# Layer 0 of a four-layer graph network on one core: the strips of the count table built in another order and at another pace

## What is computed

```
h = relu(layernorm(x));  x = x + L0(h)   # sum over edges of (h @ W[edge type])[src], 16 types, + bias + h @ W_loop
h = relu(layernorm(x));  x = x + L1(h)   # [h, sum over edges of h[src]] @ W.T + b
h = relu(layernorm(x));  x = x + L2(h)   # an MLP on every edge (h[src], h[dst], edge features), mean per node
h = relu(layernorm(x));  x = x + L3(h)   # sum over edges of [h[src], edge features] @ W1, then a last product
```

## Time and profile before

| | us |
|---|---|
| median of 3 runs (4931.5 to 4936.65) | 4932.48 |
| the profiled execution, its own time | 4949.62 |
| its span, first to last instruction | 4947.3 |
| busy in the span: PE, DVE, ACT, POOL | 3938.6, 2813.5, 2195.5, 3564.0 |
| layer 0's gathers by POOL: first start, last end | 254.2, 2138.48 |
| the count table: first quad, last quad | 463.0, 2118.7 |

### The profile page before, as it was taken

The page is one execution under the profiler, slowest core; times in us unless marked ns, Lnnn a source line. Parts: engine busy times, 40 slices in busy tenths (PEclk is TensorE's granted clock), DMA queues, the critical chain, the costliest instruction groups (busy, mean ns, idle before and its releaser), DMA issues. The chain is left out here.

```text
span 4947.3 us, 75766 instructions
## 1 busy us (share of the span) xinstructions
PE 3938.6 (80%) x24234; PEld 2678.4 (54%) x24249; DVE 2813.5 (57%) x7266; ACT 2195.5 (44%) x3840; POOL 3564.0 (72%) x3738
## 2 busy tenths in 40 slices
PE   6755677777788777749996688888889999999876
PEld 3354566555444443434543566666666666666643
DVE  7576999977666666643433332234445555666434
ACT  4510257767778888820111333333333333333300
POOL 6777577777777777757770677777777777777756
PEclk9855567878776778769997777789899999999888
DMA  8821223444344344448883323334445556666376
GB/s 278 325 55 36 55 89 121 132 134 130 122 133 132 120 146 132 135 117 294 279 274 119 85 80 80 80 108 130 122 133 146 157 165 170 175 170 177 98 212 175
DMA packets 580950, 719.66 MB, mean 145 GB/s; under 512 B 138104, under 2 KB 463580, under 8 KB 569952
## 3 DMA queue, kind: packets, MB, share of 16 engines
q1 hardware_dynamic: 394526, 509.02, 31.2%
q0 software_dynamic: 118064, 176.98, 14.9%
q10 hardware_dynamic: 67986, 28.96, 2.2%
HBM read 502.83 MB, written 217.42 MB: 146 GB/s over the span
## 5 line engine op out<-in xcount | busy, mean ns | idle before, releaser
L1356 POOL DMA_INDIRECT layer_msg<-snd_table,idx_src x1536 | 1461.3, 951 | 587.3 <-issue 458.0
L1356 POOL DMA_INDIRECT layer_msg<-rel_table,idx_rel x1440 | 1399.5, 972 | 495.2 <-issue 427.5
L1623 ACT CAST early_room<-layer_unit_ps 128x700 fp8e4<-128x700 f32 (+5 forms) x1371 | 1115.6, 884 | 483.2 <-PE layer_unit_ps L2337 368.3
L2277 PE MATMUL layer_sum_ps<-layer_sel,layer_msg 128*97 128x24 f32 (+21 forms) x6560 | 896.5, 283 | 393.1 <-DVE layer_hidden_acc L1820 150.3
L2337 PE MATMUL layer_unit_ps<-layer_hot_room,layer_low_hot 128*128 128x350 bf16 (+6 forms) x5172 | 940.9, 327 | 318.5 <-ACT early_room L1623 201.6
L2277 PEld LDWEIGHTS layer_sum_ps<-layer_sel,layer_msg 128*128 128x128 f32 (+2 forms) x6560 | 882.6, 208 | 515.5 <-issue 268.7
L2337 PEld LDWEIGHTS layer_unit_ps<-layer_hot_room,layer_low_hot 128*128 128x128 bf16 x5172 | 445.9, 124 | 732.5 <-ACT early_room L1623 550.7
L1808 DVE TENSOR_TENSOR layer_msg<-layer_pre_ps,layer_msg 128x512 f32<-128x512 f32 x392 | 270.9, 691 | 958.3 <-DMA layer_msg<-snd_table,idx_src 878.7
L1944 DVE TENSOR_SCALAR layer_hot_room<-count_iota,frame_key 128x686 bf16<-128x686 f16 (+6 forms) x2586 | 699.7, 336 | 0.0
L2260 PEld LDWEIGHTS layer_pre_ps<-layer_rcv,layer_sel_t 128*128 128x128 f32 x3144 | 476.0, 217 | 228.6 <-issue 228.6
L1356 POOL DMA_INDIRECT layer_msg<-h_table,idx_src x416 | 401.3, 965 | 181.9 <-issue 121.4
(11 more groups left out here) (290 smaller groups left out, 4028.8 us busy)
## 6 DMA issues: line engine op xcount, KB each, us to landing
counts<-early_room SPq DMA_DIRECT2D x48, 1543.5 KB
layer_unit<-counts SPq DMA_DIRECT2D x120, 441.0 KB
rel_table<-first_rows SPq DMA_DIRECT2D x98, 512.0 KB
layer_attr<-in_edge_attr_dram SPq DMA_DIRECT2D x766, 64.0 KB
layer_piece<-counts SPq DMA_DIRECT2D x24, 1575.0 KB
layer_rcv<-rcv_table SPq DMA_DIRECT2D x396, 64.0 KB
counts<-early_room SPq DMA_DIRECT2D x16, 1568.0 KB
layer_msg<-snd_table,idx_src POOLq DMA_INDIRECT x1536
```

The lines of the kernel that those rows point to most:

```text
L1356: nc.gpsimd.indirect_dma_start(msg[g][:, u, 0:2 * D if dense else width], None, of, bass.IndirectOffsetOnAxis(ap=idx[:, at:at + 1], axis=0 ...
L1623: nc.scalar.copy(to[:, :, col:col + w].rearrange("p (v h) c -> p v h c", v=2), of.rearrange("p v (h c) -> p v h c", c=w), saturate=False). ...
L2277: last = nc.tensor.matmul(sum_ps[g % 2][0:rows, 0:span], msg[g][:, u, 0:rows], sel[j][:, u, 0:span], start=u == 0, stop=u == TILES - 1)
```

## The change

Three things change, all of them in the lists that are made before the program is written out.

- `interleave` puts the strips into a new order. They are parted at strip 41 into two queues; whichever engine, DVE or ACT, has had less than its share of its own whole time so far gets strips from the queue that suits it, two at a time (strips 1 to 3 one at a time). Strip 0 stays first.
- `number` counts tiles in the new order; a tile's place in the edge lists (its slot, `SLOT_OF`) stays as it was, so that the gathers of the lists and the table in HBM are the same. A quad is now up to four tiles with neighbouring slots: 650 quads where there were 647.
- The weight of a unit comes from the time of DVE and of ACT by the two formulas.

```
+def vector_time(frames):
+    return sum(tiles * (0.37 + 0.024 * width) for width, tiles, _, _ in frames)
+
+def scalar_time(frames):
+    return 0.2 * -(-sum(width for width, _, _, _ in frames) // WIDEST) + 0.0955 * sum(f[0] for f in frames)
+
+def interleave(strips):
+    ahead, behind = list(range(1, len(strips) // 2)), list(range(len(strips) // 2, len(strips)))
+    taken = []
+    times = [[of(frames) for _, _, frames in strips] for of in (vector_time, scalar_time)]
+    whole = [sum(time[1:]) for time in times]
+    while ahead or behind:
+        spent = [sum(time[k] for k in taken) for time in times]
+        queue = behind if behind and (not ahead or spent[0] * whole[1] > spent[1] * whole[0]) else ahead
+        take = 1 if queue[0] < 4 else 2
+        taken += queue[:take]
+        del queue[:take]
+    taken.insert(0, 0)
+    return [strips[k] for k in taken]
...
-            weight = [sum(tiles * (3 * width + 11) for width, tiles, _, _ in held) +
-                      6 * sum(width for width, _, _, _ in held) + 12 for _, held in UNITS]
+            loads = [(vector_time(held), scalar_time(held)) for _, held in UNITS]
+            whole = [sum(load[e] for load in loads) for e in range(2)]
+            shares = [(load[0] / whole[0], load[1] / whole[1]) for load in loads]
+            weight = [max(0.85 * max(pair), sum(pair) / 2) for pair in shares]
...
-                    at = tiles[0] + (LIST_GAP if tiles[0] >= HEAD_TILES else 0)
+                    at = SLOT_OF[tiles[0]]
```

More of the change, by code:

```diff
@@ L99, in lay_out @@
 def lay_out():
-    panels, strips, frames, runs, node, tile, at, gap = [], [], [], [], 0, 0, 0, 0
+    panels, strips, runs, node, at, slot = [], [], [], 0, 0, 0
     for n, (cols, shapes) in enumerate(PANEL_STRIPS + TAIL_STRIPS):
         if n == len(PANEL_STRIPS):
-            node, gap = TAIL_NODE, -tile % P
+            node, slot = TAIL_NODE, -(-slot // P) * P
         panels.append((cols, len(shapes), node, at))
         for shape in shapes:
-            begin, col = len(frames), 0
+            frames, col = [], 0
             for width, tiles, count in shape:
@@ L112, in lay_out @@
                 else:
-                    runs.append((node, width, tiles, count, tile + gap))
+                    runs.append((node, width, tiles, count, slot))
                 for _ in range(count):
-                    frames.append((width, tiles, col, tile))
-                    col, node, tile = col + width, node + width, tile + tiles
+                    frames.append((width, tiles, col, slot))
+                    col, node, slot = col + width, node + width, slot + tiles
             assert col == cols <= STRIP_COLS
-            strips.append((cols, at, begin, len(frames)))
+            strips.append((cols, at, frames))
@@ L119, in lay_out @@
             at += P * HI * cols
-    return panels, strips, frames, runs, tile, at, gap
-PANELS, STRIPS, FRAMES, RUNS, COUNT_TILES, TABLE, LIST_GAP = lay_out()
+    return panels, strips, runs, at, slot
+def vector_time(frames):
[15 more added lines that the diff above has]
+    return [strips[k] for k in taken]
@@ new lines, in number @@
+def number(laid):
+    strips, frames, slots = [], [], []
+    for cols, at, held in laid:
+        begin = len(frames)
+        for width, tiles, col, slot in held:
+            frames.append((width, tiles, col, len(slots)))
+            slots += range(slot, slot + tiles)
+        strips.append((cols, at, begin, len(frames)))
+    quads = []
+    for tile, slot in enumerate(slots):
+        if quads and len(quads[-1]) < TILES and slots[quads[-1][-1]] + 1 == slot:
+            quads[-1].append(tile)
+        else:
+            quads.append([tile])
+    return strips, frames, slots, quads
@@ L124 @@
+PANELS, LAID, RUNS, TABLE, LISTED = lay_out()
+STRIPS, FRAMES, SLOT_OF, QUADS = number(interleave(LAID))
+COUNT_TILES = len(SLOT_OF)
 HEAD_PANELS = len(PANEL_STRIPS)
-HEAD_TILES = FRAMES[STRIPS[sum(len(shapes) for _, shapes in PANEL_STRIPS)][2]][3]
-HEAD_CH = (HEAD_TILES + LIST_GAP) // P
-LISTED = COUNT_TILES + LIST_GAP
+HEAD_TILES = sum(tiles * count for _, shapes in PANEL_STRIPS for shape in shapes for _, tiles, count in shape)
+HEAD_CH = -(-HEAD_TILES // P)
 def make_units():
@@ L146 @@
 UNIT_TILES = [held[-1][3] + held[-1][1] for _, held in UNITS]
-QUADS = [range(t, min(t + TILES, HEAD_TILES)) for t in range(0, HEAD_TILES, TILES)]
-QUADS += [range(t, min(t + TILES, COUNT_TILES)) for t in range(HEAD_TILES, COUNT_TILES, TILES)]
 QUAD_OF = [k for k, tiles in enumerate(QUADS) for _ in tiles]
@@ L1268, in layer_phase @@
                 share_by = min(max(q + 1 - BEGIN, 0), END - BEGIN)
-                while u < len(UNITS) and (spent + weight[u]) * (END - BEGIN) <= sum(weight) * share_by:
+                while u < len(UNITS) and (spent + weight[u]) * (END - BEGIN) <= sum(weight) * share_by + 1e-6:
                     spent += weight[u]
```

## The result

| | before | after |
|---|---|---|
| median of 5 runs, taken side by side | 4936.22 us (4931.5 to 4941.15) | 4964.64 us (4957.24 to 4971.21) |
| ratio, 95% interval | | 1.0055 (1.0043 to 1.0066) |
| the profiled execution | 4949.62 us | 4960.26 us |
| in it, POOL's waits for PE's sums in layer 0, less 0.30 us each (net) | 46 us | 94.9 - 79 x 0.30 = 71 us |
| its mean granted clock | 0.819 | 0.801 |

The change makes the kernel 0.55% slower; 4902 was forecast, and the median of after lies above the range as well. (In after's code every line of layer 0 stands 43 lower: gathers L1399, sums L2320, count matmuls L2380, evacuation L1666, adds L1863.)

The account below looks back on a forecast made before the run. Layer 0 was taken to be bound by POOL's gathers plus its waits for PE: 46 us of old loss less 16 us of new made 30 us faster, 4932.48 - 30 = 4902 us; range 4884 to 4942, its own range 4888 to 4922.

Parts of the forecast that it names:

- The stall at strip 0: POOL's waits for PE's sums, mostly 500 to 700 us in layer 0, would go: 46 us won.
- the lag behind strips 0 and 1: Lag carried into the first wide strips: 15 us (11 to 22), under the 33 us that cost nothing.
- The price of a wide step at each clock: Steps of 6.17 7-wide units: 4.9 us at 2.4 GHz, 6.25 at 1.2 GHz, against POOL's 5.09.
- The share of time at 1.2 GHz: In wide strips 41 to 82, PE at 1.2 GHz 57% of the time, adding 0.57 us of lag a step.
- the table's own working: Lag summed strip group by strip group; anything beyond 33 us is lost to POOL, 16 us in all.
- strip 2 gave back: Strip 2, between wide strips 41-52 and 53-60, was to reduce the lag by 11 us in 11 steps.
- the half clock stays: Rival: PE stays at 1.2 GHz in wide strips, 1.16 us a step, 91 us lost, 4977 us; chance 0.10.
- break-even of 74%: Share of wide-strip time at 1.2 GHz where loss equals gain: 0.82 us a step, 48 us lost.
- 0.74 a step: Upper end of the forecast's own range: 69% at 1.2 GHz in wide strips, 36 us lost, 4922 us.
- no 200 us of the wide stretches had less than 0.66: Argument against PE staying at 1.2 GHz, from mean clocks of the earlier trace's wide stretches.
- The rival of the full clock: A lagging PE holds 2.4 GHz; wide steps take 4.9 us, all 46 us come back, 4886 us; chance 0.17.
- ACT the bound at any clock: Rival: ACT at 0.868 us a 7-wide unit, 5.66 us a wide step; 59 us lost, 4945 us; chance 0.03.

Follow-up runs that it names:

- e7: After, with the first count matmul of every wide unit (one frame of 6 or 7 columns) issued twice; 4890.73 us in one run.
- e8: After, with two identity matmuls of 128 columns ahead of PE's wait for ACT at wide units in steps without node work; 4886.72 us in one run.
- e4: After, with ACT writing out only 25 of the 50 rows in each half of a wide unit; 4885.90 us in one run.
- e1_pace_only: The kernel before, old order of strips, with only the new unit weights; 4930.24 us, ratio 0.9978 to before.
- e2: After with the old unit weights put back, so new order at the old pace; 4977.15 us, ratio 1.0068 to before.
- e5: The kernel before, old order, units weighed by the slowest of PE (1.3 times its 1.2 GHz time), DVE and ACT; 4896.36 us, ratio 0.9912.
- e6: After's new order, units weighed by the slowest of PE (1.3 times its 1.2 GHz time), DVE and ACT; 4918.15 us, ratio 0.9952 to before.
- e10: The same kernel as e8, after with PE's waits filled by identity matmuls, run four times; 4901.20 us, ratio 0.9905 to before.

## Why the prediction was wrong

**The stall at strip 0: right.** It was forecast to go, and it is gone. Its worth was put a little high: of the 46 us net, 46.0 - 17 x 0.30 = 41 lay between 500 and 700 us, the rest in small waits behind. Also right was the lag behind strips 0 and 1. The first gather and the add of step 69, the first of the wide strips, and of step 106, the first behind them, in after:

```profile
603.83 0.94 POOL L1399 DMA_INDIRECT layer_msg<-rel_table,idx_rel  x1 [0.30 <-issue]
...
629.12 0.17 DVE L1863 TENSOR_TENSOR acc<-acc,layer_sum_ps 97x24 f32 x1
...
806.61 0.94 POOL L1399 DMA_INDIRECT layer_msg<-rel_table,idx_rel  x1 [1.13 <-PE layer_sum_ps L2320]
...
853.30 0.19 DVE L1863 TENSOR_TENSOR acc<-acc,layer_sum_ps 97x32 f32 x1
```

Less the 8.0 us of a group without lag, 25.3 - 8.0 = 17 us at step 69; I carried 15.

**The price of a wide step at each clock: right.** At 1.2 GHz six 7-wide units took, in after,

```profile
775.15 1.46 PE L2320 MATMUL layer_sum_ps<-layer_sel,layer_msg 128*97 128x32 f32 x8
776.42 1.35 PE L2380 MATMUL layer_unit_ps<-layer_hot_room,layer_low_hot 128*128 128x350 bf16 x4
778.15 1.49 PE L2380 MATMUL layer_unit_ps<-layer_hot_room,layer_low_hot 128*128 128x350 bf16 x4 [0.37 <-ACT early_room L1666]
779.87 1.49 PE L2380 MATMUL layer_unit_ps<-layer_hot_room,layer_low_hot 128*128 128x350 bf16 x4 [0.23 <-ACT early_room L1666]
781.16 1.40 PE L2320 MATMUL layer_sum_ps<-layer_sel,layer_msg 128*97 128x32 f32 x8
```

6.01 us, where 5.25 + 0.855 = 6.1 follows from the earlier trace rows. Over strips 41 to 52 the lag went from 17 to 46.7 - 8.0 = 39, and 19.4 - 14 x 0.30 = 15 us were lost on the way: 37 added, against 43 in the prediction for 1.2 GHz throughout. At 2.4 GHz, in one of the few such stretches, six units took 4.55 us, where the earlier trace rows had 4.59 on ACT:

```profile
1007.49 0.79 PE L2320 MATMUL layer_sum_ps<-layer_sel,layer_msg 128*97 128x32 f32 x8
...
1012.04 0.79 PE L2320 MATMUL layer_sum_ps<-layer_sel,layer_msg 128*97 128x32 f32 x8
```

**The share of time at 1.2 GHz: wrong, and it decided.** "I take their mean, 57%" was read from the earlier trace rows, stretches of the old order. In after PEclk from 700 to 1500 is 0.50, 0.62, 0.56, 0.59, so 100, 76, 88 and 82% of the time, 86% on the mean. By the table's own working that is 0.86 x 1.16 - 0.14 x 0.2 = 0.97 us a step; between 48 us lost at 0.82 and 91 at 1.16, about 67. Measured: 71, where 16 was forecast. So the sum came near with this one input put right. Its other terms were not all met: strip 2 gave back 17 us (39 at step 106, 898.93 - 869.25 - 8.0 = 22 at step 117) where 11 was forecast. The rival "the half clock stays" came, which I gave 0.10; its break-even of 74% was passed. (0.82 a step is 75% and not 74, and 0.74 a step loses 38 us and not 36; neither changes the argument.)

The argument against it was the weak one: "no 200 us of the wide stretches had less than 0.66". That was true of wide units that arrive with little lag (in before, the group whose first gather starts at 1336.83 us is added at 1351.46: 14.6 - 8.0 = 7 us) and behind strips in which the clock was up; from 823 to 922 it was at 1.00. Which of the two kept it up is not shown. The better witness was in the same group: 82 us at 0.50 with PE busy for 71 of them. The rival of the full clock, "a PE that lags always has work waiting", is refuted: from 560 to 900 us PE lagged and had 0.50. The Trainium skill, "TensorE: Matmul & The Clock Gate", Part 1, has it that activity releases the throttle. After speaks against that as far as a busy share of 90% (180.19 of 200 us) at 0.50 goes; e7 and e8 agree with it in direction, since more activity in the same strips did release it; e4, where PE's instructions were unchanged and the clock rose all the same, is a case that it does not cover.

**ACT the bound at any clock: wrong as priced, right in part.** At 2.4 GHz ACT sets the pace of the units (0.73 us each in e1_pace_only), not at the 0.868 of that rival; and at 1.2 GHz its copies are the part of the loop that e4 shortened (5.10 us for 6.01).

## What to carry to other kernels

Here the clock's share of the time could not be read in one order of the work and used in another: at the old pace, stretches with wide units had 0.66 to 0.76 in the old order and 0.51 to 0.53 in the new one (e2). So price a plan at both levels and ask if it still holds when the lower one stays. A plan that levels each step by the slowest engine, with PE priced at its slow clock (e5), took nearly the whole gain in the old order, where the clock was at 0.75 to 0.80; in the new order the same pace took about half of it (e6). In this kernel, where PE waits a little at every unit, more work on PE was a cure as well as less.

## What the runs showed of the hardware that was not expected

- In after PE's granted clock stayed at 1.2 GHz from 560 to 900 us with PE busy 83% (560 to 700) and 90% (700 to 900) of the time. 50% more columns in the wide units raised it to a mean of 0.92 from 700 to 1100 us, and a shorter ACT copy with PE's work unchanged to 0.74.
- With a filler of 2 x 128 columns a unit (e10) the clock was 1.00 from 635 to 645 us, where after had 0.50; from 705 to 760, where steps had node work and no filler, it was 0.50, and 1.00 in e7 with the same node work and its own added columns.
- Why narrow strips bring the clock up in the kernel before (1.00 from 823 to 922 us at 73 of 99 us busy) while wide ones at 90% do not, no run settles.
